# An audio tower (token, attention and feed-forward blocks) on one Trainium2 core: the token stage rebuilt around transposing transfers, and a shorter order of work in attention

## The chip, the cores and the metric

The kernel runs on one core of one Trainium2 chip. The metric is device time in microseconds (us). Three runs of the kernel before took 2093.0, 2093.45 and 2094.6 us; the median is 2093.45.

## The reference

Sixteen batches b of x (64 channels, 2048 samples) go through three blocks. P is 128, one batch gives 128 tokens of 1024 numbers.

```python
# token block
h = conv1d(x, conv_in_w, pad=3)                      # 64 -> 128 channels, 7 taps
h = gelu(groupnorm1(h, gn1_w, gn1_b))                # mean and variance over channels and samples of a batch
h = conv1d(h, dw_w, stride=2, pad=2, groups=128) + dw_b   # 5 taps, 2048 -> 1024
h = conv1d(h, pw_w)                                  # pointwise, 128 -> 128
h = gelu(groupnorm1(h, gn2_w, gn2_b))                # (16, 128, 1024)
# attention block, 32 heads, 128 tokens of each batch
n = layernorm(h)
q_c = rmsnorm(n @ w_qa, g_qa); q = q_c @ w_qb        # 384 latents; 128 + 64 rotary columns a head
kv = n @ w_kva; k_c = rmsnorm(kv[..., :128], g_kva)  # 128 latents and 64 shared rotary columns
scores = q_nope . k_nope + rope(q_rope) . rope(k_rope)
h = h + softmax(scores * 192 ** -0.5) @ v @ w_o      # k_nope and v from k_c @ w_kvb
# feed-forward block: base matrix and 8 low-rank experts, top 2
h = h + ffn(layernorm(h))
```

## The kernel before

All large products are made of three float16 products: each float32 operand is split into a high half (ScalarE, a copy with a scale) and a low half (VectorE, scaled operand minus high half), and high times high, high times low and low times high are summed in PSUM. The kernel is written engine by engine; the order on each engine is the order of the code, and semaphores tie the engines together. The three blocks run one after the other.

**Token stage** (`token_phase`, L108). `pipeline` (L64) calls a `body(i, p, ok)` on each engine for i from the first to the last pass; a part with lag n works on batch i - n. The lags are AHEAD = -2 (load and split of x), 0 (first convolution and its statistics), MID = 1 (first gelu, the five depthwise taps, pointwise product), HID = 2 (second gelu, layer norm), PROJ = 3 (turns of the hidden tile and projections to latents) and TAIL = 4 (rms norm of latents, their turns and splits). In a pass:

- TensorE: convolution chunk 0 (12 products of 512 columns, `conv`), the statistics product `stat_ps` (L609: means over the channels of batch i - 1's first norm and batch i - 2's second), four turns of hidden through the identity into `turn_ps` (L569), chunk 1, four turns, chunk 2, first half of the projections (L590, L591), chunk 3, second half, turns of the latents (L631, L633), the pointwise product (L577, which waits for the fifth tap), and the turn of the rotary keys (L640).
- GpSimd: `group_norms` (eleven dependent links of 128 x 2 on what VectorE copied from `stat_ps`), `latent_scales`, `layer_norm`, and last `x_low`, the low half of x of batch i + 2 (L326, 128 x 2054).
- ScalarE: copies of the convolution to `y1` (L232), splits of hidden (L241), gelu 1 (L261, waits for the group norms), gelu 2 (L269), the high half of x (L226), sums of squares of the projections (L281, L284), high halves of the latents, hidden itself (L303), the rotary keys (L308).
- VectorE: statistics of the second norm, the copy of `stat_ps` (L485), gains and rotary (L437 to L446), low halves of hidden from PSUM (L394), statistics of `y1` (L403), the taps (L419, L423), the norms of the latents (L459 to L465), statistics of the layer norm (L510), low halves of the latents (L394).
- SyncE's queue: the loads of x, one tile `x_f`, the next when both halves of the last have been taken.

In pass 1 the weights `wqk` are also split, a quarter behind each of the four copies of `y1`.

**Attention** (`attention_phase`, L702). 32 rounds (8 groups of 4 heads by 4 quads of batches) of 4 slots; a slot s is 4 heads of one batch. The products of the head weights for a later group are made in the slots j = 1, 2, 3 of rounds 0 to 27. TensorE's order in slot s: scores of s, latents of s - 1 (`av_ps`, probabilities times key latents), rotary queries of s + 1, queries of the next round, a product of head weights, outputs of s - 1. The probabilities of a slot are split into `halves` and turned by a transposing transfer (`turned`, L774), the rotary queries likewise (`zt`, L767). ScalarE issues the load of the head weights (L819) at the head of a round.

**Feed-forward** (`ffn_phase`): unchanged.

Of the kernel before, what the change touches and what calls it, by code (L numbers as in the profile page):

```python
# [26 lines left out]
D = T // 2  # L27
# [32 lines left out]
assert QP_S * KC_S == KR_S * QRO_S  # L60
assert HW_S * LB_S == LN_S * AW_S
# [46 lines left out]
def token_phase(nc, keep, raw_loaded, x_d, wc_d, wqk_d, pw_d, rows_d, params_d, consts_d, heads_d):  # L108


    AHEAD, MID, HID, PROJ, TAIL = -2, 1, 2, 3, 4
    LAST = B - 1
    with ExitStack() as ctx:
# [6 lines left out]
        def sem(name):  # L120
# [9 lines left out]
        ht_h, ht_l = sb("ht_h", [P, D], F16), sb("ht_l", [P, D], F16)  # L130
        q_g, k_g, k_n = sb("q_g", [P, QR]), sb("k_g", [P, KVR]), sb("k_n", [P, KVR])
        diag = sb("diag", [P, P])
        kr_a, kr_b, kr2 = sb("kr_a", [P, RD]), sb("kr_b", [P, RD]), sb("kr2", [P, 2 * RD])
        bn1, bn2, bn3 = sb("bn1", [P, 4, 6]), sb("bn2", [P, 2, 6]), sb("bn3", [P, 2, 6])
# [3 lines left out]
        msq, gv, gy, gt, c12 = (sb(n, [P, w]) for n, w in (("msq", 2), ("gv", 2), ("gy", 2), ("gt", 2), ("c12", 4)))  # L138
        st3 = sb("st3", [P, 2])
        lv, ly, lt, lc = (sb(n, [P, 1]) for n in ("lv", "ly", "lt", "lc"))  # L140
# [13 lines left out]
        (pool_passed, dve_passed, zeroed, zeroed_x, x_loaded, x_hi, x_lo, conv_done, y1_copied, bn1_done,  # L154
         st1_ready, st2_ready, stat_done, s_copied, gn_step, gelu1_done, dw_step, pw_scaled, pw_done,
         bn2_done, gelu2_done, bn3_step, ln_step, hid_done, ht_done, ht_hi, ht_lo, proj_done, ss_done,
         rms_step, rinv_done, q_taken, diag_done, kn_done, kr_step, tail1_done, tail2_done, t1_hi, t1_lo,
         kc_hi, kc_lo, t2_hi, t2_lo) = (sem(n) for n in (
             "pool_passed dve_passed zeroed zeroed_x x_loaded x_hi x_lo conv_done y1_copied bn1_done "
             "st1_ready st2_ready stat_done s_copied gn_step gelu1_done dw_step pw_scaled pw_done "  # L160
             "bn2_done gelu2_done bn3_step ln_step hid_done ht_done ht_hi ht_lo proj_done ss_done "
             "rms_step rinv_done q_taken diag_done kn_done kr_step tail1_done tail2_done t1_hi t1_lo "
             "kc_hi kc_lo t2_hi t2_lo").split())
        ZEROED = 5
        GN_STEPS, LN_STEPS, RMS_STEPS = 11, 8, 8
        params, gains, resid = keep["params"], keep["gains"], keep["resid"]
        ident = keep["consts"][:, 0:P]
# [7 lines left out]
        lags = list(range(AHEAD, TAIL + 1))  # L175
        block = ctx.enter_context(nc.Block())

        def need(eng, sem, value, most):

            if isinstance(value, int):  # L180
                value = min(value, most)
                if value <= 0:
                    return
            eng.wait_ge(sem, value)

        @block.sync
        def _(sp):
            def load(b):

                sp.dma_start(x_f[0:CI, PAD:PAD + T], x_d[bass.ds(b, 1), :, :].rearrange("a c t -> (a c) t")  # L190
                             ).then_inc(x_loaded, 16)
                sp.dma_start(x_f[CI:P, PAD - 1:PAD - 1 + T],
                             x_d[bass.ds(b, 1), :, :].rearrange("a c t -> (a c) t")).then_inc(x_loaded, 16)

            sp.dma_start(raw["wc"], wc_d).then_inc(w_loaded["wc"], 16)
            sp.wait_ge(zeroed_x, 2)
            load(0)
# [5 lines left out]
            with sp.Fori(1, B) as b:  # L203
                sp.wait_ge(x_hi, b)
                sp.wait_ge(x_lo, b)
                load(b)
# [8 lines left out]
        def _(act):  # L215
# [12 lines left out]
            def copy_y1(i, p, c):  # L228
# [5 lines left out]
                if isinstance(i, int) and i == 1:  # L234
                    weights_high("wqk", QUARTERS[c])
# [1237 lines left out]
```

## Time and profile before

| | |
|---|---|
| median of 3 runs | 2093.45 us |
| profiled execution | 2096.29 us, span 2094.5 us |
| mean granted TensorE clock | 0.975 |
| TensorE busy | 1924.3 us (92% of the span) |
| VectorE busy | 1310.3 us (63%) |
| ScalarE busy | 755.6 us (36%) |
| GpSimd busy | 286.4 us (14%) |
| token stage | first convolution product 12.61 us, last split of the rotary keys 458.38 us |
| attention | to 1856.8 us |
| feed-forward | to the end |

The span runs from the first to the last instruction of the profiled execution. Busy shares are averages over three stages with different limits, so a change of one stage is read from the rows of that stage. The granted clock is a share of full speed: 1.00 is 2.4 GHz, 0.50 is 1.2 GHz.

### The profile page before, as it was taken

What the parts mean: (1) busy time and instruction counts of PE and PEld (TensorE: products, weight loads), DVE (VectorE), ACT (ScalarE), POOL (GpSimd) and SP (SyncE); (2) the same over time, 40 slices, a digit from 0 to 9 for tenths busy, and PEclk for the clock granted to TensorE, in tenths of its full rate; (3) what the DMA queues carried; (4) which work ended last, traced back from release to release, by engine and by line L of the source; (5) the groups of instructions that cost most, each with busy time, mean ns of one, the idle gap of its engine ahead of it and who ended that gap; (6) DMA issues with size and microseconds to landing.
All of it is one profiled execution on the core that took longest, in us unless ns stands there. A gap on an engine that the chain in (4) does not pass through costs nothing. (4 is left out here: it accounts for less than half of the span.)

```text
span 2094.5 us, 33517 instructions
## 1 busy us (share of the span) xinstructions
PE 1924.3 (92%) x11794; PEld 1064.8 (51%) x11794; DVE 1310.3 (63%) x2805; ACT 755.6 (36%) x2051; POOL 286.4 (14%) x612
## 2 busy tenths in 40 slices
PE   4788888768999999999999999999999999959999
PEld 1344445444555555555555555555555555525554
DVE  2667677635666666666566665666666666665554
ACT  3444544324333333333333333333333333332221
POOL 2355554320000000000000000000000000023332
PEclk9899999879999999999999999999999999989999
DMA  5112211002332232222322223222232212243332
GB/s 139 41 41 50 53 41 39 19 26 73 75 57 57 57 63 63 55 57 57 75 57 56 54 55 73 56 57 57 66 58 57 39 38 44 41 134 81 82 81 71
DMA packets 250668, 125.27 MB, mean 60 GB/s; under 512 B 240272, under 2 KB 240528, under 8 KB 248336
## 3 DMA queue, kind: packets, MB, share of 16 engines
q1 hardware_dynamic: 246192, 94.71, 21.7%
q10 hardware_dynamic: 4320, 28.51, 4.4%
q8 instruction: 94, 1.54, 0.3%
q14 instruction: 62, 0.51, 0.1%
HBM read 56.07 MB, written 8.39 MB: 31 GB/s over the span
## 5 line engine op out<-in xcount | busy, mean ns | idle before, releaser
L1073 PE MATMUL out_ps<-m_h,ot_h 128*128 128x512 f16 x1024 | 388.2, 379 | 4.1 <-DVE ot_l L872 4.1
L1075 PE MATMUL out_ps<-m_h,ot_l 128*128 128x512 f16 x1024 | 388.1, 379 | 0.0
L1074 PE MATMUL out_ps<-m_l,ot_h 128*128 128x512 f16 x1024 | 388.1, 379 | 0.0
L922 DVE SCALAR_TENSOR_TENSOR resid<-out_ps,resid 128x512 f32<-128x512 f32 x256 | 177.0, 691 | 285.4 <-PE out_ps L1075 281.4
L787 ACT ACTIVATE ot_h<-av_ps 128x512 f16<-128x512 f32 x128 | 76.4, 597 | 744.2 <-PE av_ps L1095 744.2
L1264 POOL MEMSET fpower<- 128x1 f32 x1 | 0.1, 99 | 1405.0 <-POOLq L706 1405.0
L851 ACT ACTIVATE prob<-s_ps,nmx 128x128 f32<-128x128 f32 x512 | 180.1, 372 | 5.7 <-DVE nmx L948 5.7
L1073 PEld LDWEIGHTS out_ps<-m_h,ot_h 128*128 128x128 f16 x1024 | 100.2, 98 | 129.7 <-issue 13.4
L1074 PEld LDWEIGHTS out_ps<-m_l,ot_h 128*128 128x128 f16 x1024 | 100.2, 98 | 129.2 <-issue 18.6
L1075 PEld LDWEIGHTS out_ps<-m_h,ot_l 128*128 128x128 f16 x1024 | 100.2, 98 | 120.9
L943 DVE TENSOR_REDUCE mx<-s_ps 128x4 f32<-128x512 f32 x128 | 88.5, 691 | 74.8 <-PE s_ps L1058 74.8
L872 DVE SCALAR_TENSOR_TENSOR ot_l<-av_ps,ot_h 128x512 f16<-128x512 f32 x128 | 88.5, 691 | 70.3 <-ACT ot_h L787 70.3
L872 DVE SCALAR_TENSOR_TENSOR halves<-prob,halves 128x512 f16<-128x512 f32 x128 | 88.6, 692 | 46.4 <-ACT halves L787 46.4
L851 ACT ACTIVATION_READ_ACCUMULATOR prob<-s_ps,nmx 128x1 f32 x512 | 109.3, 213 | 0.0
L1008 PE MATMUL qp_ps<-qct_h,wp_h 128*128 128x512 f16 x378 | 104.8, 387 | 0.0
L1008 PE MATMUL qp_ps<-qct_h,wp_l 128*128 128x512 f16 x378 | 102.7, 381 | 0.0
L1008 PE MATMUL qp_ps<-qct_l,wp_h 128*128 128x512 f16 x378 | 102.1, 379 | 0.0
L787 ACT ACTIVATE halves<-prob 128x512 f16<-128x512 f32 x128 | 80.6, 630 | 51.3 <-DVE prob L956 51.3
L1377 PE MATMUL fout<-wb_l,fht_h 128*128 128x512 f16 x256 | 97.3, 380 | 0.0
L1377 PE MATMUL fout<-wb_h,fht_h 128*128 128x512 f16 x256 | 97.3, 380 | 0.0
L1377 PE MATMUL fout<-wb_h,fht_l 128*128 128x512 f16 x256 | 97.1, 379 | 0.0
L1051 PE MATMUL s_ps<-kct_h,qp_h 128*128 128x128 f16 x512 | 92.4, 219 | 0.4 <-DVE qp_l L872 0.4
(239 smaller groups left out, 4011.7 us busy)
## 6 DMA issues: line engine op xcount, KB each, us to landing
wide<-heads_in ACTq DMA_DIRECT2D x30, 928.0 KB, 5.3
wide<-x_in SPq DMA_DIRECT2D x32, 512.0 KB, 6.3
tower_out<-result SPq DMA_DIRECT2D x16, 512.0 KB, 2.6
stage<-wb_in SPq DMA_DIRECT2D x8, 512.0 KB, 8.5
resid<-wqk_in SPq DMA_DIRECT2D x1, 2304.0 KB, 12.5
zt<-z SPq DMA_TRANSPOSE x128, 2.4
turned<-halves SPq DMA_TRANSPOSE x128, 3.0
wide<-heads_in SPq DMA_DIRECT2D x2, 928.0 KB, 5.3
```

The costliest lines, as they stand in the source:

```text
L787: act.activation(out, src, ACT.Copy, scale=scale).then_inc(done, 1)
L851: act.activation(prob[:, h, :], s_ps[:, h * P:(h + 1) * P], ACT.Exp, bias=nmx[:, h:h + 1], scale=EXP_SCALE, accum_out=rsum[:, h:h + 1]).th ...
L872: dve.scalar_tensor_tensor(out=out, in0=src, scalar=scale, in1=high, op0=ALU.mult, op1=ALU.subtract).then_inc(done, 1)
L922: dve.scalar_tensor_tensor(out=resid[:, at], in0=out_ps[hf][:, :], scalar=1.0 / (O_S * M_S), in1=resid[:, at], op0=ALU.mult, op1=ALU.add). ...
L943: dve.tensor_reduce(mx[:, :], s_ps[:, :].rearrange("p (h n) -> p h n", h=HEADS), AX.X, ALU.max).then_inc(max_step, 1)
L1008: last = pe.matmul(bank[:, :], w[:, bass.ds(side, 1), k, j, :].rearrange("p a n -> p (a n)"), q[:, k, bass.ds(tok, CHUNK)], start=n == 0, ...
L1051: pe.matmul(out[h], q_h[h], k_h, start=h == 0, stop=False)
L1073: pe.matmul(out_ps[hf][:, :], ot_h[:, h, :], m_h[:, at], start=h == 0, stop=False)
L1074: pe.matmul(out_ps[hf][:, :], ot_h[:, h, :], m_l[:, at], start=False, stop=False)
L1075: last = pe.matmul(out_ps[hf][:, :], ot_l[:, h, :], m_h[:, at], start=False, stop=h == HEADS - 1)
L1264: pool.memset(power[:, :], -0.5).then_inc(powered, 1)
L1377: pe.matmul(out_ps[p][hf][:, :], h[p][:, k, :], w[:, k, hf * CHUNK:(hf + 1) * CHUNK], start=k == 0 and n == 0, stop=False)
```

## The change

The token stage is rewritten, and the order of a slot of attention is shortened.

- Lags: AHEAD is -1, there is a new lag LOW = 5 for the low halves of the latents. The first chunk of x of batch 0 (1,032 columns) is loaded and split by itself ahead of the convolution's weights.
- Hidden is split in SBUF (`hid2`, high and low half side by side, 2 x 1024 float16) and turned by one transposing transfer of 2,048 columns a batch. The latents and the rotary keys are normalised and split in SBUF (`lat2`, and `kc`) and turned by two transfers a batch. The turns on TensorE, `turn_ps`, `diag`, `k_n` and the splits out of `turn_ps` are gone, and the free PSUM bank becomes a third one for the convolution.
- TensorE's order in a pass: chunk 0, the statistics product, chunks 1, 2, 3, the pointwise product, both halves of the projections.
- GpSimd's order: `group_norms` (one link is issued without a wait behind it), `x_low`, `latent_scales`, `layer_norm`.
- VectorE takes the statistics of the second norm in the pass of the pointwise product, at its end.
- SyncE's queue is unrolled and carries the transposing transfers ahead of the load of x.
- Attention: latents of slot s come last in slot s instead of early in s + 1; outputs of s - 1 come ahead of the queries; ScalarE and VectorE split the latents at the end of the slot.

```diff
-    AHEAD, MID, HID, PROJ, TAIL = -2, 1, 2, 3, 4
+    AHEAD, MID, HID, PROJ, TAIL, LOW = -1, 1, 2, 3, 4, 5
...
-        conv_ps = [pb("conv_ps0"), pb("conv_ps1")]
-        stat_ps, turn_ps = pb("stat_ps"), pb("turn_ps")
+        conv_ps = [pb("conv_ps0"), pb("conv_ps1"), pb("conv_ps2")]
+        stat_ps = pb("stat_ps")
...
         @block.sync
+            def body(i, p, ok):
+                if ok(PROJ):
+                    b = i - PROJ
+                    sp.wait_ge(hid_lo, b + 1)
+                    need(sp, proj_done, b, B)
+                    sp.dma_start_transpose(ht[:, :, :], hid2[:, :]).then_inc(hid_turned, 16)
+                if ok(LOW):
+                    b = i - LOW
+                    sp.wait_ge(lat_lo, b * 2 + 2)
+                    sp.dma_start_transpose(lat[:, 0:8, b * P:(b + 1) * P],
+                                           lat2[:, :, :].rearrange("p a n -> p (a n)")).then_inc(lat_turned, 16)
+                    sp.wait_ge(kc_lo, b + 1)
+                    sp.dma_start_transpose(lat[:, 8:10, b * P:(b + 1) * P],
+                                           kc[:, b * 2 * P:(b + 1) * 2 * P]).then_inc(kc_turned, 16)
+                if ok(-2) and i >= -1:
+                    sp.wait_ge(x_hi, i + 2)
+                    sp.wait_ge(x_lo, i + 2)
+                    load(i + 2, 0, XW, x_loaded)
...
         @block.scalar
             def body(i, p, ok):
+                if ok(PROJ):
+                    b = i - PROJ
+                    act.wait_ge(ln_step, b * LN_STEPS + LN_STEPS)
+                    need(act, hid_lo, b, B)
+                    act.activation(hid[:, :], resid[:, b * D:(b + 1) * D], ACT.Identity, bias=lc[:, 0:1],
+                                   scale=ly[:, 0:1]).then_inc(hid_done, 1)
+                    act.wait_ge(hid_done, b + 1)
+                    need(act, hid_turned, b * 16, B * 16)
+                    act.activation(hid2[:, 0:D], hid[:, :], ACT.Copy, scale=LN_S).then_inc(hid_hi, 1)
                 if ok(0):
                     copy_y1(i, p, 0)
-                if ok(PROJ):
-                    hidden_high(i - PROJ, 0)
+                if ok(AHEAD):
+                    x_high(i - AHEAD)
...
         @block.gpsimd
             def body(i, p, ok):
                 if ok(MID) or ok(HID):
                     group_norms(i)
+                if ok(AHEAD) and i >= 0:
+                    x_low(i - AHEAD)
                 if ok(TAIL):
                     latent_scales(i - TAIL)
                 if ok(HID):
                     layer_norm(i - HID)
-                if ok(AHEAD) and (not isinstance(i, int) or i >= 0):
-                    x_low(i - AHEAD, p)
...
         @block.vector
+                if ok(PROJ):
+                    b = i - PROJ
+                    dve.wait_ge(hid_hi, b + 1)
+                    need(dve, hid_turned, b * 16, B * 16)
+                    low(hid2[:, D:2 * D], hid[:, :], LN_S, hid2[:, 0:D], hid_lo)
+                if ok(LOW):
+                    latents_low(i - LOW)
                 if ok(TAIL):
                     take_latents(i - TAIL)
...
         @block.tensor
                 if ok(0):
                     conv(i, p, 1)
-                if ok(PROJ):
-                    turn_hidden(i - PROJ, 1)
-                if ok(0):
                     conv(i, p, 2)
-                if ok(PROJ):
-                    project(i - PROJ, 0)
-                if ok(0):
                     conv(i, p, 3)
-                if ok(PROJ):
-                    project(i - PROJ, 1)
...
                 if ok(MID):
                     pointwise(i - MID)
+                if ok(PROJ):
+                    project(i - PROJ)
...
-            def latents(r, j):
...
             def body(before, now, after, more):
                 for j in range(QUAD):
                     scores(now, j, operands)
-                    if behind[0]:
-                        latents(*behind)
...
+                    if before or j:
+                        if j:
+                            outputs(now, j - 1)
+                        else:
+                            outputs(before, QUAD - 1)
                     if after:
                         queries(after, j)
                     if more and j:
                         products(now.t + HEADS, now.parity, j - 1, prod_ps, (now.t + HEADS) * 3 + (j - 1))
+                    pe.wait_ge(p_turned, s * 16 + 16)
+                    pe.matmul(av_ps[:, :], kc[:, at], probs_h, start=True, stop=False)
+                    pe.matmul(av_ps[:, :], kc[:, at_l], probs_h, start=False, stop=False)
+                    pe.matmul(av_ps[:, :], kc[:, at], probs_l, start=False, stop=True).then_inc(av_done, 1)
```

## Rows read from the trace of the kernel before

**Rows 1.** Table by stages: stretch and length (us), busy time of each engine, PEclk.
```profile
79.10:82.50 3.40, 2.96 (x4) 1.33 (x5) 3.08 (x7) 0.00 (x0) 0.43 (x2) 0.50 0.00 0
129.20:368.50 239.30, 204.83 (x1181) 115.96 (x1181) 166.61 (x350) 115.11 (x189) 130.08 (x281) 1.00 0.19 44
...
1692.30:1810.80 118.50, 118.50 (x782) 66.23 (x781) 77.91 (x168) 42.27 (x144) 0.00 (x0) 1.00 0.21 41
```

**Rows 2.** Timeline of TensorE, one pass: start, duration (us), idle before in brackets.
```profile
206.37 0.35 PE L609 MATMUL stat_ps<-st,mean_mat 128*128 128x4 f32 x2 [2.44 <-issue]
...
212.67 0.32 PE L590 MATMUL q_ps<-wqk_h,ht_h 128*128 128x384 f16 x1
...
215.61 1.03 PE L558 MATMUL conv_ps<-wide,wc_h 128*128 128x512 f16 x4
...
218.20 0.32 PE L590 MATMUL q_ps<-wqk_h,ht_h 128*128 128x384 f16 x1
...
222.08 1.88 PE L577 MATMUL pw_ps<-dw,pw 128*128 128x512 f32 x4
...
230.36 0.36 PE L609 MATMUL stat_ps<-st,mean_mat 128*128 128x4 f32 x2 [2.71 <-issue]
```

**Rows 3.** Timeline of VectorE in the same pass and the next.
```profile
214.69 5.24 DVE L423 SCALAR_TENSOR_TENSOR dw<-g,params,dw 128x1024 f32<-128x1024 f32 x4
...
229.59 0.67 DVE L411 SCALAR_TENSOR_TENSOR st<-st 128x1 f32<-128x1 f32 x1
```

**Rows 4.** Timeline of ScalarE in the same pass.
```profile
211.69 2.10 ACT L261 ACTIVATE g<-y,c 128x2048 f32<-128x2048 f32 x1 [0.76 <-POOL c L344]
...
222.12 0.19 ACT L284 ACTIVATION_READ_ACCUMULATOR junk<-kv_ps 128x1 f32 x1
...
226.24 1.24 ACT L303 ACTIVATE hid<-resid,lc,ly 128x1024 f32<-128x1024 f32 x1 [3.18 <-POOL lc L369]
```

**Rows 5.** Timeline of GpSimd in the same pass.
```profile
214.88 1.15 POOL L355 TENSOR_TENSOR nrm<-rv,ry 128x2 f32<-128x2 f32 x1 [0.18 <-POOL ry L105]
...
226.17 4.07 POOL L326 TENSOR_TENSOR x_l<-wide 128x2054 f16<-128x2054 f32 x1
```

**Rows 6.** Timeline of GpSimd and VectorE in pass 1.
```profile
37.80 4.07 POOL L326 TENSOR_TENSOR x_l<-wide 128x2054 f16<-128x2054 f32 x1 [9.42 <-ACT wide L226]
...
39.19 3.90 DVE L394 SCALAR_TENSOR_TENSOR wqk_l<-resid,wqk_h 128x1152 f16<-128x1152 f32 x1 [0.36 <-ACT wqk_h L220]
```

**Rows 7.** Timeline of TensorE, passes 1 to 3.
```profile
56.88 3.78 PE L577 MATMUL pw_ps<-dw,pw 128*128 128x512 f32 x4 [11.72 <-DVE dw L423]
...
79.54 3.43 PE L577 MATMUL pw_ps<-dw,pw 128*128 128x512 f32 x4 [5.44 <-DVE dw L423]
...
85.40 0.28 PE L609 MATMUL stat_ps<-st,mean_mat 128*128 128x4 f32 x2
```

**Rows 8.** Timeline, pass 15 and the last split of the stage.
```profile
373.52 0.36 PE L609 MATMUL stat_ps<-st,mean_mat 128*128 128x4 f32 x2 [2.26 <-issue]
...
458.07 0.28 ACT L308 ACTIVATE kr_h<-turn_ps 128x128 f16<-128x128 f32 x1 [1.42 <-PE turn_ps L640]
```

**Rows 9.** Waits from 500 to 1780 us: total (us), times, longest (us).
```profile
PEld s_ps L1057 <- DMA zt<-z: 13.7, 18, 1.9
...
PE s_ps L1057 <- DMA zt<-z: 10.2, 13, 1.7
PE av_ps L1093 <- DMA turned<-halves: 9.5, 28, 0.4
```

**Rows 10.** Timeline of TensorE, VectorE and SyncE's queue in one slot of attention.
```profile
1014.84 0.22 PE L1058 MATMUL s_ps<-kr_l,zt 128*128 128x128 f16 x1
...
1018.37 0.69 DVE L956 TENSOR_TENSOR prob<-prob,rrec 128x512 f32<-128x512 f32 x1
...
1021.33 1.23 SPq L774 DMA_TRANSPOSE turned<-halves  x1
```

**Rows 11.** Transfers of the page: times, median us to landing.
```profile
turned<-halves SPq DMA_TRANSPOSE x128, 3.0
```

More of the change, by code:

```diff
@@ L186, in _, with load @@
         @block.sync
         def _(sp):
[L188 to L193, printed above, removed]
+            def load(b, lo, hi, done):
+                xs = x_d[b:b + 1, :, :].rearrange("a c t -> (a c) t")
+                for rows, pad in ((slice(0, CI), PAD), (slice(CI, P), PAD - 1)):
+                    at = slice(max(lo - pad, 0), min(hi - pad, T))
+                    sp.dma_start(x_f[rows, at.start + pad:at.stop + pad], xs[:, at]).then_inc(done, 16)
@@ L830, in start @@
                 rope_high(0)
-            def latent_high(s, first):
-                act.wait_ge(av_done, s + 1)
-                if not first:
-                    act.wait_ge(out_done, s * 2)
-                high(ot_h[:, :, :].rearrange("p h n -> p (h n)"), av_ps[:, :], O_S / (PR_S * KC_S), o_hi)
             def body(before, now, after, more):
@@ L844, in body @@
                     s = now.slot + j
-                    if before or j:
-                        latent_high(now.slot + (j - 1), not before and j == 1)
                     act.wait_ge(max_step, s * 2 + 2)
@@ L863, in body @@
                         prod_high(now.t + HEADS, now.parity, now.side * -1 + 1, now.place, j - 1, prod_ps, False)
-                if not after:
-                    latent_high(now.slot + (QUAD - 1), False)
+                    act.wait_ge(av_done, s + 1)
+                    if before or j:
+                        act.wait_ge(out_done, s * 2)
+                    high(ot_h[:, :, :].rearrange("p h n -> p (h n)"), av_ps[:, :], O_S / (PR_S * KC_S), o_hi)
             rounds(act, start, body)
@@ L940, in body @@
                     s = now.slot + j
-                    behind = (now, j - 1) if j else (before, QUAD - 1)
                     dve.wait_ge(s_done, s + 1)
@@ L958, in body @@
                                       ).then_inc(norm_step, 1)
+                    behind = (now, j - 1) if j else (before, QUAD - 1)
                     if after or j < QUAD - 1:
@@ L968, in body @@
                         prod_low(now.t + HEADS, now.parity, now.side * -1 + 1, now.place, j - 1, prod_ps)
-                    if behind[0]:
-                        add_out(*behind, 0)
-                        add_out(*behind, 1)
+                    dve.wait_ge(o_hi, s + 1)
+                    low(ot_l[:, :, :].rearrange("p h n -> p (h n)"), av_ps[:, :], O_S / (PR_S * KC_S),
+                        ot_h[:, :, :].rearrange("p h n -> p (h n)"), o_lo)
                 if not after:
-                    latent_low(now.slot + (QUAD - 1))
                     for hf in range(2):
```

427 lines of the change are left out of this document (183 added, 244 removed).

## The prediction

> **What bounds the kernel now.** I read the table by stages first, then the timelines of one pass of the token stage engine by engine, then the start, the end of that stage, and one slot of attention. The table [rows 1] says where time can be had. In the steady token stage TensorE is busy 204.8 of 239.3 us at a granted clock of 1.00; in the last attention rounds without products it is busy 118.5 of 118.5 us, so attention is bound by TensorE's own work and the token stage is not quite. The feed-forward stage behind attention is not touched.
>
> One token pass is the distance of two statistics products on TensorE, 206.37 to 230.36 in one case and (373.52 - 85.40) / 12 = 24.0 us over twelve [rows 2, 7, 8]. Inside it the reader should see four convolution chunks of 2.59 us (215.61 to 218.20), two projection halves of 2.94 us (212.67 to 215.61), a pointwise product of 1.88 us, turns through the identity, and one idle stretch of 2.7 us before the statistics product. The clock stays full over these 2.7 us stretches [rows 1].
>
> Beside it runs a chain that begins at the statistics product: copy, eleven GpSimd links, gelu at 211.69, taps until 214.69 + 5.24 = 219.93 [rows 3, 4]. From the product to the last tap: 219.93 - 206.37 = **13.56 us**. The pointwise product waits for that tap. Now it stands behind both projection halves and starts at 222.08, 2.1 us after the tap: the chain is hidden, by the turns, three chunks and 5.9 us of projections.
>
> **The change, part by part.** Everything is summed against the profiled execution's own 2096.29 us (span 2094.5); the median of the runs shown is 2.8 us lower, and I take that off at the end.
>
> *TensorE's order.* After the statistics product TensorE has three chunks (7.8 us), then the pointwise product, which waits for the same tap, then the projections. So the projections no longer hide the chain; they are queued behind the wait. The loop is closed: statistics product, chain, pointwise, projections, first chunk of the next batch, next statistics product. Its length is 13.56 + 1.88 + 5.9 + 2.6 + 0.1 for hand-overs = 24.0 us, which is what a pass costs today. So what the change takes off TensorE (twelve turns and five small products, about 1.9 us a pass, with their wait of 0.8 us, and the 2.7 us stall) is worth nothing: it all becomes idle time ahead of the pointwise product. This is the step on which the forecast rests. The shorter GpSimd order (one link no longer waited for) gives 0.18 us back, as the links stand some 0.37 us apart.
>
> *GpSimd and VectorE on one port.* The trace shows that a GpSimd instruction and a VectorE instruction with both inputs in SBUF exclude one another. A small VectorE link that takes 0.22 us takes 0.67 us from 229.59 and ends at 230.26, when x_low (226.17 + 4.07) ends [rows 3, 5]; a split of weights that should take 1.3 us takes 3.90 us from 39.19, because x_low runs from 37.80 to 41.87 [rows 6]; and a GpSimd link of 0.19 us takes 1.15 us from 214.88, to the end of a tap [rows 5]. Today x_low runs when VectorE is idle, behind the layer norm. The change puts it right behind the group norms, and its input is cast long before. Then it starts with the gelu and runs 3.8 to 4.1 us; the gelu takes 2.1 us, so the taps start 1.7 to 2.0 us late: **+1.9**. And the low half of hidden is no longer taken from PSUM in two pieces, but from SBUF, 1,024 columns, as long as a tap (5.24 / 4 = 1.31 us). It waits for ScalarE: squares until 222.31, 1.2 us behind the projections' end at 221.14, then hid (1.24 us) and its high half (about 1.1), so it starts some 3.5 us behind the projections [rows 4]. The group-norm links start at 3.4 us (2.6 for the chunk, 0.8 for the product and the copy). They stand still for most of 1.31 us: **+1.0** (0 if they win each time, 1.3 at most). Chain: 13.56 - 0.18 + 1.0 + 1.9 = 16.3 us. Behind them on VectorE stand taps, bn3, bn2 of the pass, which end some 4 us before the next statistics product needs them.
>
> *The clock.* TensorE then idles 16.3 - 8.0 = 8.3 us a pass. After idle stretches of 11.72 and 5.44 us the pointwise product took 3.78 and 3.43 us for 1.88 [rows 2, 7], and the granted clock there was 0.50, the 1.2 GHz level [rows 1]. So each pass starts its product and part of its projections at half speed: at least 3.43 - 1.88 = 1.55 us, and 1.90 plus what is left for the work behind it, some 2.6; I take **+2.0**. By the Trainium skill, "TensorE: Matmul & The Clock Gate", section "Loop structure matters more than you think", a long idle wait in each turn of a loop lets the clock fall to half each time and the matmuls behind it run cold; the trace agrees, with the two products above.
>
> A pass: 16.3 + 1.9 + 5.9 + 2.6 + 0.1 + 2.0 = **28.8 us** for 24.0. Twelve of them: **+57 us**. Bounds: 24.0 - 0.2 + 1.55 = 25.4 with no port wait, 29.8 with the dear values.
>
> *Transfers.* The transposing transfer of 1,024 columns lands in 3.0 us [rows 11]; for the 2,048 of hidden I take 4.2, at most 6. It starts 5 us into the pass and is wanted at 18: hidden by the chain; without that cover it would cost some 2 us. Those of the latents are wanted passes later. The next x load is queued behind them on SP and is issued when x_low is done, 13 us into the pass; with 7 us for landing it has 8 us to spare. The removed evictions and the third bank for the convolution lie in idle time and count nothing.
>
> *Start.* The first pointwise product waits until 56.88 [rows 7], because the group norms stand behind x_low of batch 2, which waits for its load (37.80) [rows 6]. Now they stand ahead of it, and the first product starts from a chunk of x, some 3 us earlier. Walking the queues with these durations I get the last tap of batch 0 at 45.7 instead of 56.7, and, after the two new waits of the next pass, the statistics product of pass 3 at 75 instead of 85.40: **-10** (-16 to -5).
>
> *End of the stage.* From the statistics product of pass 15 to the end there are 458.35 - 373.52 = 84.8 us [rows 8]. New: one pass without x_low and chunks, twice 24.5, then norms 12.6, a wait for projections in ScalarE's order, hidden and its transfer 9, projections at half clock 9, latents, one more pass for their low halves and two transfers: about 97. **+12** (+3 to +16).
>
> *Attention.* Latents of a slot now wait for their own slot's probabilities. Last score product 1014.84, normalisation 1018.37, transfer issued 1021.33, 3.0 us to landing [rows 10, 11]: from scores' end (1014.90) to data is 9.4 us today. The reordering lets the maximum begin 0.1 later and the normalisation 0.45 sooner (no high half of the latents before the exponentials), so 8.7 to 9.0. TensorE has rope 0.98, outputs 24 x 0.2157 = 5.18, queries 9 x 0.2157 = 1.94, and products of 0 to 0.87: cover 8.1 to 9.0. The wait is about 0.75 in slots without a product and 0.1 in others: some 0.85 a round, 23 us in 27 rounds, and 9 in the 12 slots behind them, which take 118.5 / 12 = 9.87 now [rows 1]. Against it, the waits for zt and turned, 10.2 + 13.7 + 9.5 = 33.4 us [rows 9], come from the load of head weights that is issued with the transfers; it would now be issued at the end of a slot and be over before them, so they go. First slot, last round and end: +6. Sum **+5** (-15 to +40: below, if the wait is nil; above, if a wait of 0.3 in each slot comes on top). The Trainium skill, "Advanced Engine Details and Errata", section "X-Bar Transpose (TRN2)", expects 350 to 400 GB/s of a transposing transfer; for 256 KB that would be 0.7 us by an estimate from the page, no latents would wait, and attention would come out some 39 us lower; the row says 3.0, and I go by it.
>
> **Sum.** -10 + 57 + 12 + 5 = +64: 2096.3 + 64 = 2160, less 2.8: **2157 us**.
>
> **Rivals.**
> *Only one of the two extra prices.* The serial order is as above, but the port waits or the clock's fall stay away: 25.4 to 26.8 a pass, +17 to +34, with start, end and attention near +3: 2110 to 2135. For it: the order in which two engines take the port is seen only in a few places. Against: all the cases shown, in both directions, point one way [rows 3, 5, 6].
> *TensorE becomes the bound (the other side).* If the last tap came within 8 us of the statistics product, TensorE would never wait: 4 x 2.59 + 5.9 + 1.9 + 0.2 = 18.4 us a pass, -67 in twelve, 2020 us. It decides in our favour from a chain of 13.0 us at full clock, where the sum is zero. For it: the profile's idle time on every other engine. Against: the chain is 13.56 today and nothing in it is made shorter but one link.
> *Attention pays for its short order.* The transfer is late in every slot, 0.5 us or more beyond my wait: +60 and more, 2190 and up. Against: the cover above.
> *Nothing comes of it.* Start and attention pay for a pass of about 24.5: 2093.
>
> **How the numbers follow.** The forecast 0.62 (2135 to 2185), one price only 0.17 (2108 to 2135), attention's price 0.07 (above 2185), TensorE's bound or a milder gain 0.11 (2020 to 2089), nothing 0.03. A measurement here tells 0.2%, 4 us. Slower 0.62 + 0.17 + 0.07 = 0.86, same 0.03, faster 0.11. The range 2108 to 2185 leaves 0.07 above and 0.14 below out.
>
> **What would show it.** Right: idle time of 7 to 9 us on TensorE before each pointwise product, put down to the taps; clock 0.50 behind it; taps that start when x_low ends; passes of 28 to 29 us; 0.6 to 1 us before latents in slots without products. Wrong: passes near 24 or 18 us, x_low and taps side by side, a clock of 1.00 in the token stage.

## The result and the profile after

The changed kernel took **2129.4 us** (2128.8, 2129.4 and 2130.5); the kernel before took 2093.45. The ratio is 1.016 (95% interval 1.0139 to 1.0182): slower by 1.4 to 1.8 in 100. Of the profiled execution the span is 2127.6 us, where it was 2094.5, so 33.1 us more. The prediction said 2157, slower, range 2108 to 2185: inside the range, 28 us too high.

Lines of the page of the changed kernel: TensorE's busy time, the granted clock in 40 slices, and of the groups (busy, mean ns of one, idle before and its releaser) the pointwise product:

```profile
PE 1907.2 (90%) x11538; PEld 1037.4 (49%) x11538; DVE 1320.5 (62%) x2742; ACT 773.2 (36%) x2020; POOL 308.2 (14%) x596
...
PEclk9888888878999999999999999999999999979999
...
L570 PE MATMUL pw_ps<-dw,pw 128*128 128x512 f32 x64 | 58.7, 1071 | 132.2 <-DVE dw L441 132.2
```

132.2 us of idle time stand ahead of one small product, all of it put down to the last tap. The table by stages says the same of the steady token stage, of the stretch between a pointwise product and the next statistics product, and of the last attention rounds (columns as in [rows 1]):

```profile
76.00:413.90 337.90, 244.64 (x1225) 127.42 (x1224) 200.74 (x358) 135.37 (x201) 174.94 (x317) 0.86 0.32 66
...
204.60:214.90 10.30, 10.30 (x57) 6.15 (x58) 4.68 (x12) 1.90 (x7) 2.35 (x10) 0.84 0.01 2
1716.70:1839.80 123.10, 120.80 (x781) 65.12 (x780) 79.65 (x169) 44.09 (x146) 0.00 (x0) 1.00 0.21 39
```

TensorE is busy 72 in 100 of the stage, at a granted clock of 0.86, where it was busy 86 in 100 at 1.00 [rows 1]. Twelve passes take 413.92 - 76.02 = 337.9 us, 28.16 each, against 24.0 before. One pass on TensorE (compare [rows 2]):

```profile
188.59 0.28 PE L599 MATMUL stat_ps<-st,mean_mat 128*128 128x4 f32 x2
...
204.60 3.56 PE L570 MATMUL pw_ps<-dw,pw 128*128 128x512 f32 x4 [7.94 <-DVE dw L441]
213.88 1.03 PE L561 MATMUL conv_ps<-wide,wc_h 128*128 128x512 f16 x4
...
216.47 0.28 PE L599 MATMUL stat_ps<-st,mean_mat 128*128 128x4 f32 x2
```

From the statistics product to the pointwise there are 16.0 us, 7.9 of them idle; the product takes 3.56 us for 1.88; projections and the first chunk follow, and the loop closes. Where the 33 us are, by statistics products, the first score product and the last output product of attention (the last row of stretches runs from the one to the other):

| stretch | before | after | difference | predicted |
|---|---|---|---|---|
| start to statistics product of pass 3 | 85.4 | 76.0 | -9.4 | -10 |
| twelve passes | 288.1 | 337.9 | +49.8 | +57 |
| pass 15 to first score | 107.3 | 115.2 | +7.9 | +12 |
| attention, from there | 1375.6 | 1360.6 | -15.0 | +5 |
| sum | | | +33.3 | +64 |

Now the two waits on the port, of GpSimd and of VectorE in the next pass:

```profile
217.53 1.06 POOL L348 TENSOR_TENSOR msq<-s,msq 128x2 f32<-128x2 f32 x1 [0.18 <-POOL msq L347]
...
222.52 3.82 POOL L335 TENSOR_TENSOR x_l<-wide 128x2054 f16<-128x2054 f32 x1
```

```profile
217.31 1.23 DVE L412 SCALAR_TENSOR_TENSOR hid_hl<-hid,hid_hl 128x1024 f16<-128x1024 f32 x1 [0.36 <-ACT hid_hl L275]
...
224.73 2.16 DVE L437 TENSOR_SCALAR dw<-g,params 128x1024 f32<-128x1024 f32 x1 [2.74 <-ACT g L288]
226.92 5.25 DVE L441 SCALAR_TENSOR_TENSOR dw<-g,params,dw 128x1024 f32<-128x1024 f32 x4
```

A GpSimd link of two columns takes 1.06 us and ends at 218.59, as the low half of hidden ends on VectorE (217.31 + 1.23 = 218.54); the link behind it is long too (218.79 to 219.16) and ends with the next low half (219.06). The first tap takes 2.16 us, and the second starts at 226.92, behind the end of the low half of x (222.52 + 3.82 = 226.34). The profile's spans on GpSimd are rough, so differences of some tenths are not to be pressed.

In attention no line of the list of waits names zt or turned any more [rows 9], and no slot takes 13.8 us. What is left of the wait for turned stands there as "issue": 28.2 us in 87 times ahead of the latents' first weight load, where the kernel before had 13.6 in 30. A slot without products takes 10.05 us instead of 9.87, one with the last product 10.80 instead of 10.73. And there is a wait that the kernel before did not have, once a round, ahead of the first score product:

```profile
PEld s_ps L1009 <- DVE qp_l L835: 12.2, 29, 1.0
```

It is for the low half of the round's queries. In the new order only the products of head weights and the latents stand between the last queries and the next scores; in rounds 28 to 30, which have no such products, the last slot takes 10.80 us instead of 9.87.

### The profile page after: what moved, and what is told of

The parts are those of the page before. It is cut to its first block and busy times, and to the rows that moved or that the text cites. A ratio compares the mean times of both kernels' runs of the same rounds, so it can differ in the third digit from the quotient of the medians.

```text
span 2127.6 us, 32412 instructions
## 1 busy us (share of the span) xinstructions
PE 1907.2 (90%) x11538; PEld 1037.4 (49%) x11538; DVE 1320.5 (62%) x2742; ACT 773.2 (36%) x2020; POOL 308.2 (14%) x596
## 5 line engine op out<-in xcount | busy, mean ns | idle before, releaser
L756 ACT ACTIVATE qp_h<-qp_ps 128x512 f16<-128x512 f32 x126 | 75.2, 597 | 491.7 <-PE qp_ps L966 491.7
L835 DVE SCALAR_TENSOR_TENSOR qp_l<-qp_ps,qp_h 128x512 f16<-128x512 f32 x126 | 87.2, 692 | 233.8 <-ACT qp_h L756 233.8
L966 PE MATMUL qp_ps<-lat,wp_h 128*128 128x512 f16 x756 | 204.6, 379 | 0.0
L570 PE MATMUL pw_ps<-dw,pw 128*128 128x512 f32 x64 | 58.7, 1071 | 132.2 <-DVE dw L441 132.2
L982 PE MATMUL rope_ps<-wr_h,lat 128*128 128x256 f16 x768 | 127.1, 275 | 0.0
L966 PEld LDWEIGHTS qp_ps<-lat,wp_h 128*128 128x128 f16 x756 | 74.1, 98 | 89.9 <-issue 1.1
L812 ACT ACTIVATION_READ_ACCUMULATOR prob<-s_ps,nmx 128x1 f32 x512 | 103.8, 203 | 0.0
L966 PE MATMUL qp_ps<-lat,wp_l 128*128 128x512 f16 x378 | 102.1, 379 | 0.0
```

Source lines behind the costliest of these rows:

```text
L570: pe.matmul(pw_ps[hf][:, :], keep["pw"][:, :], dw[:, hf * CHUNK:(hf + 1) * CHUNK], start=True, stop=True).then_inc(pw_done, 1)
L756: act.activation(out, src, ACT.Copy, scale=scale).then_inc(done, 1)
L812: act.activation(prob[:, h, :], s_ps[:, h * P:(h + 1) * P], ACT.Exp, bias=nmx[:, h:h + 1], scale=EXP_SCALE, accum_out=rsum[:, h:h + 1]).th ...
L835: dve.scalar_tensor_tensor(out=out, in0=src, scalar=scale, in1=high, op0=ALU.mult, op1=ALU.subtract).then_inc(done, 1)
L966: last = pe.matmul(bank[:, :], w[:, bass.ds(side, 1), k, j, :].rearrange("p a n -> p (a n)"), q[:, k, bass.ds(tok, CHUNK)], start=n == 0, ...
L982: last = pe.matmul(rope_ps[:, 0:HEADS * RD], q[:, k, bass.ds(tok + j * P, P)], w[:, bass.ds(side, 1), k, :].rearrange("p a n -> p (a n)"), ...
```

## The experiments

Theory: the place of the pointwise on TensorE makes the chain a closed loop with the projections; the port and the clock add their prices to it; in attention the load of head weights gives the gain, and the shorter order costs something. The rivals stand with each run. A kernel's pass length is (statistics product of pass 15 minus that of pass 3) / 12. Ratios are to the kernel before, with intervals; medians of it were 2094.5, 2095.7 and 2096.7 us in the three groups of four.

| run | us | ratio (95%) | pass |
|---|---|---|---|
| project_first | 2040.2 | 0.9735 (0.9707 to 0.9762) | 21.6 |
| x_low_split | 2122.1 | 1.0127 (1.0098 to 1.0155) | 27.5 |
| both_moves | 2081.0 | 0.9932 (0.9909 to 0.9955) | 25.1 |
| filled_wait | 2102.1 | 1.0035 (1.0022 to 1.0047) | 26.2 |
| attention_as_before | 2146.2 | 1.0234 (1.0203 to 1.0265) | 28.2 |
| zt_first | 2147.1 | 1.0239 (1.0208 to 1.0271) | 28.1 |
| load_later | 2068.3 | 0.9855 (0.9823 to 0.9886) | 24.8 |
| pointwise_ahead | 2162.6 | 1.0308 (1.0277 to 1.0340) | 29.1 |
| split_sooner | 2027.6 | 0.9667 (0.9645 to 0.9689) | 20.6 |
| first_and_later | 2025.2 | 0.9658 (0.9637 to 0.9679) | 21.5 |
| all_three | 2012.5 | 0.9593 (0.9572 to 0.9615) | 20.5 |
| filled_and_split | 2090.9 | 0.9973 (0.9962 to 0.9983) | 25.2 |

**The order on TensorE.**

```diff
-                if ok(MID):
-                    pointwise(i - MID)
                 if ok(PROJ):
                     project(i - PROJ)
+                if ok(MID):
+                    pointwise(i - MID)
```

> One thing moved back in the changed kernel: TensorE takes the projections ahead of the pointwise convolution, so they lie under the taps again. If the place of the pointwise in TensorE's order is what lengthened the pass, the projections' 5.9 us leave the path between taps and statistics product. What is left there is the chain of 15.85 us and then VectorE: from its last tap to the finished statistics it took 5.3 us (232.17 to 237.5), longer than pointwise and first conv chunk warm (4.5). A pass of 21.3 us, up to 22 if the low half of hidden now falls on more of GpSimd's links; the idle time before the pointwise falls from 7.9 to about 2 us, and the granted clock stays at 1.00. Twelve passes of 28.16 become 258 us: about 2051 us (2043 to 2062). Rival: the transposing transfer of hidden lands too late, and the projections wait for it ahead of the pointwise: a pass of 24 or more, 2080. Rival: the order is not what costs, 2129.

It took 2040.2 us, 89 less than the changed kernel and 3 below the expected range. TensorE in one pass, and its pointwise product in another:

```profile
243.81 1.98 PE L570 MATMUL pw_ps<-dw,pw 128*128 128x512 f32 x4 [1.89 <-DVE dw L441]
249.19 0.36 PE L599 MATMUL stat_ps<-st,mean_mat 128*128 128x4 f32 x2 [0.80 <-issue]
...
265.44 3.30 PE L570 MATMUL pw_ps<-dw,pw 128*128 128x512 f32 x4 [2.23 <-DVE dw L441]
```

The wait is some 2 us (1.6 to 2.2) instead of 7.9. In eight of the twelve passes the product is at full clock; in the other four it takes 3.1 to 3.4 us, the granted clock of the 2 us behind its start is 0.60 to 0.69, and the pass is longer by about 1 us. 12 x (28.16 - 21.59) = 79 us come from the passes, 9 from the end of the stage. It is the order that costs: with it swapped the other parts of the token stage's change are together a gain, 24.0 to 21.6 us a pass. The transfer of hidden is not late.

The converse, on the kernel before (the turns left where they are):

```diff
-                    project(i - PROJ, 0)
...
                     conv(i, p, 3)
+                if ok(MID):
+                    pointwise(i - MID)
                 if ok(PROJ):
+                    project(i - PROJ, 0)
                     project(i - PROJ, 1)
```

> The kernel before with one thing of the change alone: on TensorE conv chunk 3, then the pointwise, then both halves of the projections. The pass is then 13.56 + 0.1 from statistics product to last tap, and behind it in TensorE's order pointwise 1.88, projections 5.9, turns 0.9 and conv chunk 2.6: 24.9 us instead of 24.0, 2093 + 11 = 2104 us (2098 to 2110), if the clock holds over TensorE's idle time ahead of the pointwise of about 4.7 us. Rival: that idle time drops the clock, another 2 us in each pass: 2128. Rival: the order alone costs nothing (the chain of the other engines sets the pass): 2093.

It took 2162.6 us, and the pass is 29.1 us: more than the forecast and its dearest rival had. The chain was as computed, 13.6 us from statistics product to pointwise; the clock fell, though the wait was only 4.54 us; and there is a wait that neither theory had:

```profile
227.95 0.30 PE L639 MATMUL turn_ps<-consts,kr 128*128 128x128 f32 x1 [1.89 <-DVE kct_l L394]
...
244.43 3.45 PE L577 MATMUL pw_ps<-dw,pw 128*128 128x512 f32 x4 [4.54 <-DVE dw L423]
```

The same turn in the kernel before:

```profile
224.76 0.30 PE L640 MATMUL turn_ps<-consts,kr 128*128 128x128 f32 x1 [0.80 <-DVE kct_l L394]
```

The pointwise had stood between the last turns and had covered most of the eviction that the turn of kr waits for (0.8 us of it was left, now 1.9). 24.9 + 1.9 = 26.8, and with 2.0 for the clock, a price that filled_wait below measures in the changed kernel and no run measured here, 28.8 of the 29.1 us.

**The port.** GpSimd's low half of x in two pieces, the second at the end of its pass (the waits for it count to two per batch):

```diff
                 if ok(AHEAD) and i >= 0:
-                    x_low(i - AHEAD)
+                    x_low(i - AHEAD, 0)
...
                     layer_norm(i - HID)
+                if ok(AHEAD) and i >= 0:
+                    x_low(i - AHEAD, 1)
```

> The changed kernel with GpSimd's low half of x in two pieces: columns up to 1032 where it stands now, the rest at the end of GpSimd's pass; the order on TensorE as changed. The first piece should take about 1.95 us (half of 3.82) and end inside the GELU (2.1 us). If VectorE's first tap waits for GpSimd's long subtraction, that tap falls from 2.16 to about 0.83 us, the taps end 1.35 us sooner, and the pass goes from 28.16 to 26.8 us: 2113 us (2108 to 2118). Rival: the first tap is long for another reason (it reads what ScalarE has just written), and nothing moves: 2129. Rival: the second piece comes so late that the load of x behind it holds up the next conversion: over 2129.

It took 2122.1 us, 4 above the expected range. The steady pass (4 to 15) is 27.3 us. VectorE's taps:

```profile
249.98 0.81 DVE L440 TENSOR_SCALAR dw<-g,params 128x1024 f32<-128x1024 f32 x1 [2.74 <-ACT g L288]
250.82 5.25 DVE L444 SCALAR_TENSOR_TENSOR dw<-g,params,dw 128x1024 f32<-128x1024 f32 x4
```

The first tap takes 0.81 us, and the distance from statistics to pointwise falls from 15.88 to 14.40. The port wait is shown, as a price of 1.35 us on a tap. But the steady pass gained only 0.9 of 1.48 us (28.20 in the changed kernel, 27.27 here), and the interval behind the statistics product of pass 3 was 30.2 us. In that one pass the next load of x was issued just ahead of the transposing transfer of hidden, and ScalarE, whose cast of x stands ahead of the gelu, waited for it:

```profile
75.28 1.10 SPq L195 DMA_DIRECT2D wide<-x_in  x2
77.11 5.00 SPq L202 DMA_TRANSPOSE ht<-hid_hl  x1
...
82.59 1.91 ACT L255 ACTIVATE wide<-wide 128x2054 f16<-128x2054 f32 x1 [6.33 <-DMA wide<-x_in]
```

The transfer's issue held SyncE's queue for 5.00 us (1.7 to 3.1 in all later passes). That is the third rival of the expectation, in one pass of twelve, and it comes back in every pass of both_moves below.

**The clock.** Thirty products without use between conv chunk 3 and the pointwise:

```diff
+                if ok(0) and ok(MID):
+                    pe.wait_ge(s_copied, i)
+                    for _ in range(30):
+                        pe.matmul(stat_ps[:, 8:CHUNK], wc_h[:, 0, :], x_h[p][:, 8:CHUNK], start=True, stop=True)
                 if ok(MID):
                     pointwise(i - MID)
```

> The changed kernel with 30 products of 128 x 504 columns (their result is not used) between conv chunk 3 and the pointwise, so that TensorE has no long idle time there; they take 30 x 0.21 = 6.3 of the 7.9 us. If the lower granted clock is a price of its own, the clock stays at 1.00, the pointwise takes 1.88 instead of 3.56 us, and the pass falls by the 1.5 us that pointwise, projections and conv chunk lose now: 26.6 us, 2111 us (2106 to 2116). Rival: the slow stretch costs nothing on the path, 2129. Rival: the 1.5 us are not the clock but contention on TensorE's operands, 2129 or more with the clock at 1.00.

```profile
264.26 6.54 PE L608 MATMUL stat_ps<-wide,wc_h 128*128 128x504 f16 x30
272.11 1.98 PE L570 MATMUL pw_ps<-dw,pw 128*128 128x512 f32 x4 [1.31 <-DVE dw L441]
```

```profile
73.20:387.10 313.90, 297.01 (x1585) 153.61 (x1586) 200.82 (x358) 136.98 (x203) 175.12 (x317) 1.00 0.35 71
```

More work made the kernel 27 us quicker than the changed one, 4 below the expected range. The clock is 1.00 over the stage; the distance from statistics to pointwise stayed 15.88 us on average, and the rest of the pass fell from 12.28 to 10.28. The clock costs **2.0 us a pass**, as the prediction had it; the 1.5 of the expectation, read off one pass of the changed kernel, was too little.

> X_low_split with TensorE's wait ahead of the pointwise filled by 24 products whose result is not used. x_low_split had shortened the chain by 1.48 us and the pass by only 0.86, and filled_wait the pass by 2.0. If the missing 0.6 us are the clock (a longer stretch at 0.50 behind the shorter wait), they come back when the wait is filled: the pass is 28.16 - 1.48 - 2.0 = 24.7 us, 12 passes give 42 us: 2087 us (2082 to 2092). Rival: the second piece of x_low holds the pass up behind the pointwise: 25.3 us, 2094.

24 such products on top of the split: 2090.9 us, the steady pass 24.73, against 26.14 with the products alone: with the clock full the split gives 1.41 of its 1.48 us. So the missing 0.6 us of x_low_split were the clock. A chain made shorter brought the pointwise earlier, but the slow stretch went on behind it: in x_low_split the pointwise takes 3.78 us, and the granted clock of the 5.9 us behind its start is 0.55 (0.73 in the changed kernel, 204.60 to 210.50):

```profile
256.10:262.00 5.90, 5.88 (x16) 2.81 (x17) 5.31 (x12) 1.11 (x3) 3.19 (x11) 0.55 0.02 4
```

The 4 us of distance to the expected 2087 are again the interval behind pass 3 (30.3 us), with the same order of the two transfers: load of x issued at 74.54, transfer of hidden at 76.30, held for 5.47 us.

**The two together, and a transfer that came in the way.**

> Projections ahead of the pointwise, and the low half of x in two pieces. If the two prices are apart and add, the chain is 14.4 us and VectorE's 5.3 us follow: a pass of 19.8 to 20.6 us, and 2129 - 12 x (28.16 - 20.2) = 2034 us (2028 to 2042), below the kernel before by 3 in 100. Rival: VectorE or GpSimd is then the bound in the stage at about 21.5 us, and the second move gives nothing on top of the first: 2051.

A miss by 47 us: 2081.0, worse than the first move alone. ScalarE in one pass, and SyncE's queue in the same pass (its duration is the time that an issue held the queue):

```profile
258.88 1.91 ACT L255 ACTIVATE wide<-wide 128x2054 f16<-128x2054 f32 x1 [7.31 <-DMA wide<-x_in]
260.70 0.58 ACT L261 ACTIVATE y<-conv_ps 128x512 f32<-128x512 f32 x1
261.18 2.09 ACT L288 ACTIVATE g<-y,c 128x2048 f32<-128x2048 f32 x1
```

```profile
250.87 1.10 SPq L195 DMA_DIRECT2D wide<-x_in  x2
252.65 5.67 SPq L202 DMA_TRANSPOSE ht<-hid_hl  x1
```

The second piece of the low half of x ends GpSimd's pass, at 250.80; only then is the load of the next x issued, 1.8 us ahead of the transposing transfer of hidden, and the two run together. ScalarE, whose cast of x stands ahead of the gelu, waits 7.3 us; the gelu starts 4.1 us after GpSimd's last norm link (257.04). The cover that the prediction had counted for this load (8 us) was there in the changed kernel, and the experiment had taken it away. The mending puts the piece ahead of the layer norm:

```diff
                     latent_scales(i - TAIL)
+                if ok(AHEAD) and i >= 0:
+                    x_low(i - AHEAD, 1)
                 if ok(HID):
                     layer_norm(i - HID)
```

> As both_moves, with one step moved: the second piece of the low half of x stands behind GpSimd's latent scales and ahead of its layer norm. In both_moves the load of x was issued about 5 us later, its landing met the transposing transfer of hidden, and ScalarE waited 7.3 us for x ahead of the GELU. With the piece at its new place the load is issued about at the last tap's end, as before the move, and lands before ScalarE wants it; the layer norm starts about 0.6 us later, which the next pass hides. A pass of 20.2 to 20.6 us against 21.6 in project_first: 2040 - 14 = 2026 us (2020 to 2032). Rival: the load is not what held both_moves up, and this stays at 2081. Rival: the piece delays the layer norm, and hidden comes late: 2040 or more.

2027.6 us and a pass of 20.6, as computed. ScalarE still waits 1.6 us for x, and in the pass looked at the gelu starts 0.6 us behind the last norm link instead of 4.1.

**Attention.** Its old order on all engines behind the changed token stage:

> The changed kernel with its token stage, and the attention stage in the order that it had before on all engines (only the addresses of the latents follow the new layout). From the first score to the end the changed kernel takes 15 us less than the kernel before; if the order in the attention stage gives that, this one takes 2129 + 15 = 2144 us (2140 to 2150), with the waits for zt and the slots of 13.8 us back. Rival: the gain comes with the latents' layout or with the state in which the token stage leaves the weights, and not with the order: 2129.

2146.2 us, 17 more than the changed kernel, with 14.06 and 13.79 us slots and these waits:

```profile
PEld s_ps L1026 <- DMA zt<-z: 13.9, 22, 2.2
...
PE s_ps L1026 <- DMA zt<-z: 9.6, 15, 2.0
PE av_ps L1062 <- DMA turned<-halves: 9.2, 26, 0.4
```

Which part of the order gives it? In the kernel before, with the load alone moved:

```diff
-                if more and (not now.known or now.t + HEADS + 1 < NH):
-                    act.wait_ge(prod_done, now.t * 3 + 3 * HEADS)
-                    act.wait_ge(wr_lo, now.t + HEADS)
-                    load(now.t + HEADS + 1, 1 - now.parity)
...
                         latent_high(now.slot + (j - 1), not before and j == 1)
+                    if j == 0 and more and (not now.known or now.t + HEADS + 1 < NH):
+                        act.wait_ge(prod_done, now.t * 3 + 3 * HEADS)
+                        act.wait_ge(wr_lo, now.t + HEADS)
+                        load(now.t + HEADS + 1, 1 - now.parity)
```

> The kernel before, with the load of the head weights moved on ScalarE from the head of its round to behind the first high half of the latent output, as the new order has it by itself. If the attention stage's 15 us are the load falling into the transfers of the turned weights and zt (33.4 us of waits in the kernel before), they go here too: 2093 - 15 = 2078 us (2074 to 2088). Rival: the gain is that of the shorter order, and the load only moves its collision elsewhere: 2093.

2068.3 us: nearly twice the gain expected. Of the transfers' waits one line is left, 1.1 us in all:

```profile
PE av_ps L1093 <- DMA turned<-halves: 1.1, 2, 0.6
```

The load's issue on ScalarE's queue, and the next two on SyncE's:

```profile
665.96 0.33 ACTq L819 DMA_DIRECT2D wide<-heads_in  x1
...
669.78 1.40 SPq L767 DMA_TRANSPOSE zt<-z  x1
671.37 1.23 SPq L774 DMA_TRANSPOSE turned<-halves  x1
```

The load, which lands in 4.5 us, starts 3.8 us ahead of zt. In the kernel before, two rounds of the same stretch have it at 652.49 and 694.93, with zt at 652.53 and 694.97: 0.04 us ahead, so that both transposing transfers run beside it.

Attention takes 1345.9 us, 29.7 less than before, with 9.87 us in nearly every first slot. (In this profile the token stage, which was not touched, took 9 us longer up to the first score; its medians are 27 us below those of the kernel before, so I put no weight on these 9.) The load's move is worth 30 us, and the change's attention got 15 out of it: the rest of the shorter order would be a loss of 15 us, which first_and_later below tests.

Then its price. SyncE issues turned ahead of zt in the changed kernel; the order of before put back, in the changed kernel (with it the queue takes its two waits ahead of an issue one by one, as before; those lines are left out):

```diff
             turn_rope(0)
+            turn_rope(1)
             turn_prob(0)
-            with sp.Fori(1, ROUNDS * QUAD) as s:
-                turn_rope(s)
+            with sp.Fori(1, ROUNDS * QUAD - 1) as s:
+                turn_rope(s + 1)
                 turn_prob(s)
+            turn_prob(ROUNDS * QUAD - 1)
```

> The changed kernel with one thing of the attention stage back: SyncE issues the transposing transfer of the next slot's zt ahead of that of the turned weights, not behind it. The prediction had priced the shorter order with 0.75 us of wait for the turned weights in a slot without products; measured were 0.18. If that is because the turned transfer is issued about 0.1 us after its source is ready and not behind zt's issue of 1.2 to 1.5 us, the wait comes back: 0.57 us in the 27 + 16 slots without products, and part of it in the others: 2129 + 25 = 2154 us (2140 to 2200). Rival: the issue order is nothing, since zt's source is ready long before, and the wait stays 0.18: 2129.

2147.1 us, 18 more. Queue and source, first of the changed kernel, then of this one:

```profile
1069.83 1.23 SPq L745 DMA_TRANSPOSE turned<-halves  x1
1071.50 1.19 SPq L737 DMA_TRANSPOSE zt<-z  x1
...
1069.03 0.69 DVE L835 SCALAR_TENSOR_TENSOR halves<-prob,halves 128x512 f16<-128x512 f32 x1 [0.36 <-ACT halves L756]
```

```profile
1085.62 1.19 SPq L736 DMA_TRANSPOSE zt<-z  x1
1086.99 1.23 SPq L743 DMA_TRANSPOSE turned<-halves  x1
...
1085.75 0.69 DVE L835 SCALAR_TENSOR_TENSOR halves<-prob,halves 128x512 f16<-128x512 f32 x1 [0.36 <-ACT halves L756]
```

Source ready to issue: 1069.72 to 1069.83, 0.11 us; with zt first 1086.44 to 1086.99, 0.55 us, of which zt's issue holds the queue for 0.37, until 1086.81. What is left, 0.18 for 0.11, bounds what the waits taken one by one can cost. The slot without products goes from 10.05 to 10.49 us, by the same 0.44, and the nine slots behind round 27 that had taken 10.01 to 10.14 us pay it too (now 10.46 to 10.58).

**The versions that follow.** Project_first, with load_later's attention stage:

> The changed kernel's token stage with the projections first, and the attention stage in the order of before with the load of head weights behind the first high half. project_first took 2040 us. Load_later took 1346 us from the first score to the last output product, and the changed kernel 1361: the shorter order would then be a price of 14 us by itself, and this kernel takes 2026 us (2020 to 2030). Rival: the attention stage of load_later was that quick for another reason, and this takes 2040 or more.

2025.2 us, as expected; from first score to last output product 1345.8, against 1359.8 in project_first: the shorter order by itself is a loss of 14 us. And with the split as in split_sooner:

> Split_sooner and the attention stage of first_and_later together. If the three add: 2129 - 89 - 14 - 14 = 2012 us (2004 to 2020). Rival: split_sooner gives nothing, and this is first_and_later's 2026.

**2012.5 us**, 4.1 in 100 below the kernel before and 5.5 below the changed one. One pass of it:

```profile
241.62 0.36 PE L602 MATMUL stat_ps<-st,mean_mat 128*128 128x4 f32 x2 [0.80 <-issue]
...
256.75 1.98 PE L573 MATMUL pw_ps<-dw,pw 128*128 128x512 f32 x4 [0.69 <-DVE dw L444]
262.12 0.36 PE L602 MATMUL stat_ps<-st,mean_mat 128*128 128x4 f32 x2 [0.80 <-issue]
```

TensorE waits 1.5 us in 20.5.

## Why the prediction was right, and where its sizes were off

*The order on TensorE* was the step on which the forecast rested, and it was right: what leaves TensorE becomes idle time ahead of the pointwise, and the projections queue behind it. Pointwise_ahead shows it from one side (24.0 to 29.1 us a pass), project_first from the other (28.2 to 21.6). Project_first also shows what the prediction said only by half: the rest of the token stage's change is worth nothing in this order, but some 2.4 us a pass in the other. No run takes the turns out alone.

*The port.* The links stood still as predicted: from statistics product to gelu there are 222.60 - 216.47 = 6.1 us, where 211.69 - 206.37 - 0.18 = 5.1 were left without them, **+1.0**. The taps' term was too high: I let them start when the low half of x ends, +1.9. Measured is a first tap of 2.16 us for 0.81, **+1.35**: the tap is issued when the gelu is done and the second follows 0.6 us behind the end of x_low, so that 0.26 us of the first tap's own 0.81 run inside the wait (it ends 0.55 us behind x_low, at 226.89). The Trainium skill, "SBUF — State Buffer", section "SBUF: two separate sides", says that of a GpSimd instruction and a VectorE instruction that has two inputs in SBUF or runs in a two-port mode the one who comes first keeps the port for its whole instruction and the other is blocked fully. The tap has one such input; its mode stands in no trace. If the rule holds for it, the whole time from the tap's issue to the end of x_low, 226.34 - 224.73 = 1.61 us, would be added, and the row says 1.35. The term came out 0.55 us too high, more than the whole difference between a chain of 16.3 and 15.88 us; x_low_split shows it by itself.

*The clock.* +2.0 predicted, 2.0 measured by filled_wait. The Trainium skill, "TensorE: Matmul & The Clock Gate", section "Loop structure matters more than you think", says that the loop nest decides whether matmuls stay warm, and its good case has them back to back; the granted clock of 0.86 without and 1.00 with the useless products agrees.

*A pass*: 28.16 for 28.8. *The start*: -9.4 for -10. *The end of the stage*: +7.9 for +12; that sum had been walked in coarse steps, and I did not look further into which one was too long.

*Attention* is the term with the largest error, **-15 for +5**: a gain where a small loss was forecast, at the edge of the range stated for it. The gain was sized well: 33.4 us of waits named, 29.7 measured in load_later. The mis-sized term is the wait for turned, 0.75 us predicted in a slot without products and 0.18 measured. Its working took 2.96 us from normalisation to issue from [rows 10], and in that row zt's issue stands ahead of turned on SyncE. The change turns these two round, and the prediction has no term for it: an issue that is moved on SyncE's queue counts. Zt_first puts 0.44 us of the 0.57 back. So instead of a price of 38 us the shorter order had one of 15. The 9 us that it had put on the twelve slots of rounds 28 to 30 were 4.8 (118.4 to 123.2), and 2.8 of these come from a wait that it did not name, that of the last slot for the low half of the queries (10.80 for 9.87).

*The rivals.* One extra price only, 2110 to 2135, contains the time, but is not what happened: both prices are there, and the lower time comes from attention. TensorE as the bound was false here and is nearly true of all_three.

## What to carry to other kernels

Where a loop closes over several engines, an in-order queue decides which work hides a chain: put what is ready ahead of what waits, and read from the profile what each engine has queued behind its longest wait. Freed time on such an engine shows up as nothing until that order is right. A load that is issued early enough for its own user can still cost most as a neighbour of short transposing transfers on the path; try where it is issued before reordering the compute around them.

## What the runs showed of the hardware that was not expected

- From pass 3 on every pointwise product of pointwise_ahead, with 4.5 us or more of idle time ahead of it, took 3.4 to 3.8 us instead of 1.88. With 1.6 to 2.2 us ahead of it (project_first) it did so in four passes of twelve, at a granted clock of 0.60 to 0.69, and not in the order of the length: 0.69 behind 1.96 us (330.05), 1.00 behind 2.24 (179.13).
- A shorter wait can give back less than its length: of 1.48 us taken off the chain some 0.6 went into a longer stretch at the lower clock (x_low_split), and filling the wait with 6.5 us of useless products gave 2.0 us a pass.
- The issue of the transposing transfer of hidden held SyncE's queue for 5.67 us when a load of x (two of 512 KB) had been issued 1.8 us ahead of it (both_moves; 5.00 and 5.47 in one pass each of x_low_split and filled_and_split), against 1.94 us in project_first.
- A load of 928 KB, issued 3.8 us instead of 0.04 us ahead of a transposing transfer, changed attention by 30 us in 27 rounds (load_later). Its own landing took 4.5 us.
